# Another order for the first attention: values behind the second scores, latent scores next to the next masks, output product behind the value projection

## The reference

```python
scores = einsum('bhnqd,bhnkd->bhnqk', qb, kb) * scale          # 16 heads
attn = softmax(where(allowed, scores, NEG)); local = einsum('bhnqk,bhnkd->bhnqd', attn, vb)
pooled = x.reshape(B, nlat, chunk, D).mean(axis=2)
lscores = einsum('bhsd,bhld->bhsl', rq, rk) * lscale           # 4 latent heads
lattn = softmax(where(lat_allowed, lscores, NEG)); lat_out = einsum('bhsl,bhld->bhsd', lattn, rv)
remote = lat_out @ rout_w + rout_b
gate = sigmoid(local @ gl_w + remote_h @ gr_w)
x = x + (gate * local + (1.0 - gate) * remote_h) @ out_w + out_b
```

## Time and profile before

| | |
|---|---|
| median of 3 runs | 1472.7 us (1472.42 to 1475.72) |
| the profiled execution | 1474.58 us |
| its span, first to last instruction | 1472.8 us |
| PE busy | 1406.9 us, 96% of the span |
| PEld busy | 1064.6 us, 72% |
| DVE busy | 1092.7 us, 74% |
| ACT busy | 899.9 us, 61% |
| POOL busy | 813.5 us, 55% |

### The profile page before, as it was taken

The page is one execution under the profiler, slowest core; times in us unless marked ns, Lnnn a source line. Parts: engine busy times, 40 slices in busy tenths (PEclk is TensorE's granted clock), DMA queues, the critical chain, the costliest instruction groups (busy, mean ns, idle before and its releaser), DMA issues. The chain is left out here.

```text
span 1472.8 us, 57209 instructions
## 1 busy us (share of the span) xinstructions
PE 1406.9 (96%) x22238; PEld 1064.6 (72%) x22238; DVE 1092.7 (74%) x3032; ACT 899.9 (61%) x1573; POOL 813.5 (55%) x1145
## 2 busy tenths in 40 slices
PE   6999999999999999996999999999999959999997
PEld 4777777777777777774777777777777736766774
DVE  6777777777777777764477777877777768999986
ACT  2555555555555655553667676666767537778874
POOL 3455445554455544553377787777777743433442
PEclk9999999999999999998999999999999979999999
DMA  5500000000000000000300000000000000100111
GB/s 164 158 2 1 0 0 0 0 0 0 0 0 0 0 0 0 1 2 14 113 17 15 21 14 21 14 21 14 21 15 14 3 1 16 37 33 31 36 36 43
DMA packets 31207, 32.40 MB, mean 22 GB/s; under 512 B 3937, under 2 KB 29602, under 8 KB 31138
## 3 DMA queue, kind: packets, MB, share of 16 engines
q1 hardware_dynamic: 31138, 31.46, 6.9%
HBM read 23.06 MB, written 8.39 MB: 21 GB/s over the span
## 5 line engine op out<-in xcount | busy, mean ns | idle before, releaser
L1077 POOL TENSOR_SCALAR_AFFINE_SELECT a_probs_t<-a_probs_t 128x512 f32<-128x512 f32 x256 | 161.9, 666 | 62.6 <-ACT a_probs_t L709 62.6
L1613 DVE TENSOR_REDUCE c_neg_max<-score_banks 128x8 f32<-128x512 f32 (+1 forms) x128 | 116.6, 952 | 82.7 <-PE score_banks L1346 82.7
L1778 POOL TENSOR_SCALAR_AFFINE_SELECT c_probs_t<-c_probs_t 128x512 f32<-128x512 f32 x256 | 153.3, 634 | 14.9 <-ACT c_probs_t L1540 14.4
L1091 POOL TENSOR_TENSOR a_less<-a_attn,a_remote 128x512 f32<-128x512 f32 x31 | 39.5, 1274 | 214.3 <-DVE a_attn L884 214.3
L709 ACT ACTIVATE a_probs_t<-score_banks 128x2048 f32<-128x2048 f32 x64 | 120.2, 1878 | 47.4 <-PE score_banks L554 47.4
L1540 ACT ACTIVATE c_probs_t<-score_banks 128x2048 f32<-128x2048 f32 x64 | 120.2, 1878 | 26.4 <-PE score_banks L1374 26.4
L397 PE MATMUL side_banks<-a_xn_t,a_w_qk 128*128 128x256 f32 x512 | 134.2, 397 | 1.6 <-ACT a_xn_t L654 0.7
L861 DVE TENSOR_REDUCE a_neg_max<-score_banks 128x8 f32<-128x512 f32 (+1 forms) x128 | 116.4, 951 | 5.9 <-PE score_banks L524 5.9
L397 PEld LDWEIGHTS side_banks<-a_xn_t,a_w_qk 128*128 128x128 f32 x512 | 92.9, 196 | 12.9 <-issue 2.3
L2206 POOL TENSOR_TENSOR r_hn<-rz_t,half_hn 128x256 f32<-128x256 f32 x32 | 23.3, 729 | 138.9 <-ACT rz_t L2034 138.9
L664 ACT ACTIVATE a_k_z<-side_banks,a_b_k,row_half 128x256 f32<-128x256 f32 x128 | 61.7, 562 | 53.8 <-PE side_banks L397 53.8
(11 more groups left out here) (271 smaller groups left out, 3898.5 us busy)
## 6 DMA issues: line engine op xcount, KB each, us to landing
x_sb<-in_x SPq DMA_DIRECT2D x32, 256.0 KB, 2.9
ctx_in<-in_ctx SPq DMA_DIRECT2D x32, 256.0 KB, 2.7
out<-y SPq DMA_DIRECT2D x32, 256.0 KB, 2.1
w_ih<-in_ffn_w_ih SPq DMA_DIRECT2D x1, 768.0 KB, 4.8
w_hh<-in_ffn_w_hh SPq DMA_DIRECT2D x1, 768.0 KB, 6.2
a_raw_qk<-in_attn_qk_w SPq DMA_DIRECT2D x1, 512.0 KB, 3.8
a_raw_cross<-in_xattn_qk_w SPq DMA_DIRECT2D x1, 512.0 KB, 5.0
b_ih<-in_ffn_b_ih SPq DMA_DIRECT2D x1, 384.0 KB, 6.5
```

The costliest lines, as they stand in the source:

```text
L1077: nc.gpsimd.affine_select(out=probs, in_=probs, pattern=[[0, 4], [1, 128]], compare_op=ALU.is_ge, fill=0.0, base=-1, channel_multiplier=-1 ...
L1613: ins = nc.vector.tensor_reduce(neg_max[:, tt, :].rearrange("p (i s l) -> p i s l", i=4, s=2)[:, :, :, late], all_scores[:, :, :, 128 * (1 ...
L1778: nc.gpsimd.affine_select(out=heads, in_=heads, pattern=[[0, 4], [1, 128]], compare_op=ALU.is_ge, fill=0.0, base=0, channel_multiplier=-1) ...
```

## The change

Four streams are written in another order; one VectorE function is cut in three, and one part of it moves to GpSimd. No instruction's size changes, and none is added or dropped but semaphore and register work.

- PE, end of a step: values(prev, 0) goes ahead of transpose_x(following), project_v(at, 1) goes behind mix_transpose(old), project_out(old) follows it, and lat_scores(at) is last, next to the masks of the next step's scores.
- VectorE: lat_center is cut. lat_mask stays at the end of the step, now behind add_to_x; lat_top (the maximum) runs in the next step after normalise(old, 0); lat_norm moves behind row_max(prev, 1) and max_parts(prev, 1).
- GpSimd: lat_shift(prev), the subtraction, between bias_x(old) and less_remote(old).
- ACT: exp_lat moves behind copy_max(prev, 0); the last three copies of a step run as copy_mix, evac_av, copy_xn instead of copy_xn, evac_av, copy_mix.

```diff
--- before.py
+++ after.py
@@ -629,18 +629,18 @@
                 if prev.real:
                     lat_values(prev)
                     scores_t(prev, 1)
-                if at.real:
-                    project_v(at, 1)
+                if prev.real:
+                    values(prev, 0)
                 if following.real:
                     transpose_x(following)
-                if prev.real:
-                    values(prev, 0)
                 if old.real:
                     mix_transpose(old)
                 if at.real:
-                    lat_scores(at)
+                    project_v(at, 1)
                 if old.real:
                     project_out(old)
+                if at.real:
+                    lat_scores(at)
 
             pe.wait_ge(ident_made, 2)
             transpose_x(At(0, 0))
@@ -735,13 +735,12 @@
 
             def step(at):
                 prev, old, following = at.back(), at.back(2), at.back(-1)
-                if prev.real:
-                    exp_lat(prev)
                 if old.real:
                     copy_remote(old)
                     evac_av(old, 1)
                 if prev.real:
                     copy_max(prev, 0)
+                    exp_lat(prev)
                 if at.real:
                     evac_k(at)
                 if prev.real:
@@ -756,12 +755,12 @@
                 if prev.real:
                     copy_lat_out(prev)
                     exp(prev, 1)
+                if old.real:
+                    copy_mix(old)
+                if prev.real:
+                    evac_av(prev, 0)
                 if following.real:
                     copy_xn(following)
-                if prev.real:
-                    evac_av(prev, 0)
-                if old.real:
-                    copy_mix(old)
 
             copy_xn(At(0, 0))
             act.wait_ge(lat_loaded, 16)
@@ -826,20 +825,16 @@
                 nc.vector.tensor_tensor(v_heads[at.par][:, tt, :, 0:HD + 1], heads(v_bank[tt][:, 0:VW], HD + 1),
                                         heads(b_v[:, 0:VW], HD + 1), ALU.add).then_inc(v_ready, 1)
 
-            def lat_center(at):
+            def lat_mask(at):
                 dve.wait_ge(ls_filled, at.count(1, 1))
                 nc.vector.tensor_tensor(lat_masked[:].rearrange("p h t l -> p t h l"),
                                         two_banks[:, :, 0:LH * LAT].rearrange("p t (h l) -> p t h l", l=LAT),
                                         mask_lat[:].unsqueeze(1).to_broadcast([128, 2, LH, LAT]), ALU.add).then_inc(ls_step, 1)
+
+            def lat_top(at):
                 dve.wait_ge(ls_step, at.count(3, 1))
                 nc.vector.tensor_reduce(lat_max[:].rearrange("p h t -> p (h t)"),
                                         lat_masked[:].rearrange("p h t l -> p (h t) l"), AX.X, ALU.max).then_inc(ls_step, 1)
-                dve.wait_ge(ls_step, at.count(3, 2))
-                wait(dve, lexp_done, at.count(1, 0))
-                nc.vector.tensor_tensor(lat_s[:].rearrange("p h t l -> p (h t) l"),
-                                        lat_masked[:].rearrange("p h t l -> p (h t) l"),
-                                        lat_max[:].rearrange("p h t -> p (h t)").unsqueeze(2)
-                                        .to_broadcast([128, 2 * LH, LAT]), ALU.subtract).then_inc(ls_step, 1)
 
             def lat_norm(at):
                 dve.wait_ge(lexp_done, at.count(1, 1))
@@ -966,9 +961,10 @@
                 if old.real:
                     normalise(old, 0)
                 if prev.real:
-                    lat_norm(prev)
+                    lat_top(prev)
                     row_max(prev, 1)
                     max_parts(prev, 1)
+                    lat_norm(prev)
                 if old.real:
                     normalise(old, 1)
                     gate_logits(old)
@@ -991,8 +987,6 @@
                     x_moments()
                 if following.real:
                     pool_tokens(following)
-                if at.real:
-                    lat_center(at)
                 if at.off == 0:
                     remote_columns()
                 if old.last:
@@ -1002,6 +996,8 @@
                     cross_stats(1)
                 if old.real:
                     add_to_x(old)
+                if at.real:
+                    lat_mask(at)
 
             nc.vector.memset(w_rout[:], 0.0).then_inc(zeroed, 1)
             x_stats(At(0, 0))
@@ -1084,6 +1080,14 @@
                 nc.gpsimd.tensor_tensor(x_bias[:], x_pair(at), b_out[:].unsqueeze(1).to_broadcast([128, 2, D]),
                                         ALU.add).then_inc(xb_ready, 1)
 
+            def lat_shift(at):
+                pool.wait_ge(ls_step, at.count(3, 2))
+                wait(pool, lexp_done, at.count(1, 0))
+                nc.gpsimd.tensor_tensor(lat_s[:].rearrange("p h t l -> p (h t) l"),
+                                        lat_masked[:].rearrange("p h t l -> p (h t) l"),
+                                        lat_max[:].rearrange("p h t -> p (h t)").unsqueeze(2)
+                                        .to_broadcast([128, 2 * LH, LAT]), ALU.subtract).then_inc(ls_step, 1)
+
             def less_remote(at):
                 pool.wait_ge(attn_ready, at.count(2, 2))
                 pool.wait_ge(remote_ready, at.count(1, 1))
@@ -1111,6 +1115,8 @@
                 prev, old, second = at.back(), at.back(2), at.back(-2)
                 if old.real:
                     bias_x(old)
+                if prev.real:
+                    lat_shift(prev)
                 if old.real and not old.last:
                     less_remote(old)
                 if prev.real:
```

## The result

The changed kernel takes 1458.66 us in the median of 4 runs (1458.56 to 1459.16), the kernel before 1472.56 (4 runs, 1472.34 to 1475.72). The ratio is 0.990, with an interval of 0.9886 to 0.9914: 13.9 us less. Forecast were 1463.1 and a range from 1459.0 to 1471.5. The executions of the kernel before lie at two levels, near 1472.6 and near 1475.7, so its median moves between 1472.6 and 1475.7 from one set of executions to the next with the share of each.

A forecast was written before the change was run, and what follows sets the result against it. PE was taken to set the step length. Gains of 0.38 us less 0.06 for mixed_x gave 0.32 a step, 9.6 us over 30 steps, so the median of 1472.7 becomes 1463.1 us; range 1459.0 to 1471.5.

The forecast's parts named there:

- L442, shape: PE, end of step: 1.02 us now with a shape change in front; 0 to 0.05 gained, taken as 0.03.
- L597, shape: PE, end of step: 1.93 us now with a change and a stop in front; 0 to 0.11 gained, taken 0.05.
- L453, wait for copy_mix: PE, end of step: the wait for ScalarE's copy_mix goes; 0 to 0.22 us gained, middle 0.11 taken.
- L581, wait for add_to_x: PE, next step: x_done comes 0.6 us earlier, so L581 cannot wait; 0 to 0.1 in one of two steps, uncounted.
- L589, wait for mixed_x: PE at the mix transposes: cover for GpSimd's mixed_x nearly spent, any delay a PE wait one for one; 0.06 us charged.
- First and last steps count as nothing: Whole loop: only pairs 2 to 31, 30 steps, were counted as gaining, 9.6 us in all.
- the tie that was forecast: GpSimd, ahead of the masks: L1091 ends at 302.38, the exponential holds the masks to 302.35; slip 0.03 to 0.1 us.
- Rival 1: Latent chain makes mixed_x 0.3 us later than counted, PE's wait at L589 equals the gain, 1472.7 us; chance 0.14.
- Rival 2: Same chain well past its point: mixed_x 0.8 us late gives 1487 us, 0.5 late gives 1478; chance 0.06.
- Rival 3: Instruction stream, not tile shape, makes PE's gaps; only copy_mix's 0.11 less 0.06 is left, 1471 us; chance 0.05.
- Rival 4: All upper bounds on PE and no wait: 0.46 to 0.57 us a step, 1459 to 1456 us; chance 0.07.
- The rule: GpSimd contends with two-SBUF-input VectorE instructions, 0.18 us per overlap; no charge for the moved subtraction beside the PSUM-reading row maximum.

The follow-up runs named there:

- masks-first kernel: Kernel after with the latent masking put back ahead of add_to_x on VectorE: 1474.5 us, ratio 0.9995 to the kernel before.
- The PE order alone: Kernel before with the new order of PE and ScalarE copies, lat_center left whole on VectorE behind add_to_x: 1494.19 us, ratio 1.0133.
- the latent part alone: Kernel after with the old order of PE and of the ScalarE copies: 1476.83 us, ratio 1.0021 to the kernel before.
- the subtraction twice: Kernel after with GpSimd doing the latent subtraction a second time into an unread tile: 1478.64 us, ratio 1.0032 to the kernel before.
- the last rounds: Side-by-side repetition on one chip: kernel after 1458.55 us, with mixed_x made on VectorE 1455.45, with fewer PE waits as well 1451.19.
- the one change more: Kernel after with values(prev, 0) moved behind the transposes of x, one more tile-shape change on PE: 1461.61 us, ratio 0.9912.
- mixed_x on VectorE: Kernel after with the gate product and last sum of mixed_x moved from GpSimd to VectorE: 1455.1 us, repeated at 1455.45.

## Why the prediction was right in kind and short in size

Point by point, forecast and found, per step:

| term | forecast | found |
|---|---|---|
| L570 | 0 | 0 (1.01 and 1.01) |
| L391, shape | 0.04 | 0.04 (0.53 to 0.49) |
| L589, shape | 0.15 | 0.15 (0.59 to 0.44) |
| L442, shape | 0.03, bounds 0 and 0.05 | 0.10 (1.02 to 0.92) |
| L597, shape | 0.05, bounds 0 and 0.11 | 0.06 (1.92 to 1.86) |
| L453, wait for copy_mix | 0.11, bounds 0 and 0.22 | 0.13 (0.76 to 0.63) |
| L581, wait for add_to_x | not counted, 0 to 0.1 in one of two | 0.06 (0.88 to 0.82) |
| L589, wait for mixed_x | -0.06 | -0.05 (0.51 + 0.47 against 0.49 + 0.44) |
| sum | 0.32 | 0.49 |

- **The step that failed** is the term of L442. Its upper bound, 0.05, was carried over from the 128-column transposes L391 and L589, as "some 0.05 behind" a change. Behind a change the value projection loses 0.10: it has 1.08 of busy time in one row of after and 1.18 in the earlier trace rows, and this in every kernel of the table by its neighbour in front. A bound taken from groups of another size was no bound. L442 alone is 0.07 of the 0.17 that were missing, 2 of 5 us.
- **The second term** is L581. The prediction named the mechanism and put it aside as "not counted". The masks-first kernel shows it is real: x_sb is what L581 waits for as soon as it is late. In the earlier trace rows alone it can't be seen; VectorE's add_to_x, which was not among the rows, ended 0.15 before L581 started. In the other step L581 came 0.06 behind x_sb, so both steps were tight. Counted at 0.06 a step it is 2 us, and the range would have reached down to 1457.
- **A third term** is "First and last steps count as nothing". While the pipeline fills, PE waits for row maxima that in the kernel before stand behind the whole lat_center:

```profile
26.67 0.44 PE L518 MATMUL score_banks<-a_mask,a_mask_to 32*64 32x128 bf16 x16 [3.89 <-DVE a_neg_max L861]
```

and in the kernel after behind the mask alone:

```profile
26.11 0.32 PE L518 MATMUL score_banks<-a_mask,a_mask_to 32*64 32x128 bf16 x16 [2.05 <-DVE a_neg_max L856]
```

The third step starts at 64.53 before and at 62.67 after, 1.9 us that the forecast did not have. The PE order alone, without the cut, starts it at 65.0, the latent part alone at 60.3. One execution each was profiled, and the first step's start differs by 0.7 between two of the kernel after, so the size is rough.
- **The small ones**: 0.01 at L597, 0.02 at L453, 0.01 less wait. No run separates shape from wait at these two groups. L453 lost its wait for copy_mix and changed both neighbours; L597 lost the change in front and the stop together, and where L589 starts behind a stop and no change it takes 0.49 too (the subtraction twice), as behind a change.
- **The sum.** 30 times 0.49 would be 14.7 us. Counted out in the two traces, the 29 steps from the third start to the last lose 13.4, the filling 1.9 and the rest 0.1: the 15.4 that the profiled execution lost (1474.58 to 1459.16). The medians lost 13.9, and in the last rounds 17.0 (1475.54 to 1458.55).
- **The chain was right to a tenth.** mixed_x was to end 16.33 to 16.40 us into the shown step and PE to come at 16.41 (290.92 taken off the prediction's times); found were 16.28 and 16.38 (300.23 and 300.33 less 283.95). The subtraction took 1.04 (forecast 1.05 to 1.27). The masks L1073 start 11.40 and 11.17 us into the two steps (forecast 11.4 to 11.5). In the second the row names the exponential; in the first the exponential ends at 295.19 and L1095 at 295.24, the tie that was forecast. VectorE did not wait for the exponential: the latent sum L841 follows L868 at once. evac_k ended 0.6 before ScalarE's next work, so the displaced exponential cost nothing.
- **The rivals.** Rival 1, the chain takes it back: did not happen, but doubling the subtraction shows how near it was, 20 us for 1.1. Rival 2, slower: its price holds, its condition was not met. Rival 3, the stream and not the shape: refuted by the one change more. Rival 4, more comes free, had 0.46 to 0.57 a step and 1459 to 1456: this is what came, 0.49 and 1458.66, though with a wait of 0.05, a term above its bound and one that had been left out. Its chance of 0.07 was too little.
- **The rule.** Under the row maximum, which reads PSUM, the subtraction on GpSimd took 1.04, as a moved operation without any charge would. The Trainium skill, GPSIMD Engine Reference, section Key points, lays contention to VectorE instructions with two SBUF inputs; by that no charge was due, and the trace agrees. Its other sentence, that VectorE is about twice as fast on elementwise work, holds at 1.04 against 0.69 only in direction, and it didn't decide: the subtraction on VectorE was 18 us slower, for it stood in the chain there.

## What to carry to other kernels

Order the groups of an in-order PE stream so that equal tile shapes stand together, and price each change on both sides: in the rows of this case at 2.4 GHz, 0.09 us for the group ahead of the change, and for the group behind it 0.05 with 128 columns and 0.10 with 272. When a group moves to the end of a step, look at what shares its consumer's queue: here the order of two VectorE operations, the sum ahead of the masking, was worth 16 us. A saving ahead of a wait without room comes back as waiting, so give its chain to an idle engine first and shorten the stream after.

## What was not expected of the hardware

- A change of tile shape costs twice. Four 128-column transposes take 0.44 us start to start between equal shapes, 0.49 behind a change, 0.53 ahead of one, 0.59 between two. Four products of 272 columns take 0.92, 1.01 ahead of a change (L484), and 1.02 behind a change from 32x128 tiles (L442). The groups of 32 small products paid nothing that shows: L570 has 1.01 with every pair of neighbours, where PE does not stop behind it.
- Waits that are long satisfied can cost time on PE. With two of three left out the slot of L538 fell from 0.18 to 0.08, and with one left out and one put last that of L442 from 1.16 to 1.07. It depends on the place: the 0.18 is 0.30 in one step of two and 0.07 in the other, and in the PE order alone, where PE stops ahead of the second scores, it is 0.07 in both with all the waits. Why is not shown. Left out or reordered, with mixed_x out of the way, they brought 4.3 us (1455.45 to 1451.19).
- A wait that ends just as PE arrives is not shown as idle time. Against mixed_x on VectorE it costs the kernel after 0.04 us in the group in front and 0.06 at its own start in one step of two, and 0.01 in the other. The timeline named this wait where it was 0.47 or more (the subtraction twice, or on VectorE), and not where it was 0.1.
